# A Newton iteration with its cube formed from the other stationary operand, and without its symmetric step

## What is computed

```python
def iterative_inv(mat, n_iter=6):
    I = jnp.eye(m)
    K = mat
    denom = jnp.max(jnp.sum(K, axis=-2), axis=-1)[:, :, None, None]
    V = jnp.swapaxes(K, -1, -2) / denom
    for _ in range(n_iter):
        KV = jnp.matmul(K, V)
        V = jnp.matmul(0.25 * V, 13 * I - jnp.matmul(KV, 15 * I - jnp.matmul(KV, 7 * I - KV)))
    return V
SV = jnp.matmul(jnp.matmul(kernel1, iterative_inv(kernel2)), jnp.matmul(kernel3, V))
```

## Time and profile before

| what | value |
|---|---|
| median of three executions | 2761.87 us (2761.23 to 2764.32) |
| the profiled execution, its own time | 2772.52 us |
| its span, first to last instruction | 2770.8 us |
| TensorE matmul busy | 2229.7 us, 80% of the span |
| VectorE busy | 1893.1 us, 68% |
| ScalarE busy | 914.3 us, 33% |
| GpSimd busy | 797.3 us, 29% |
| mean granted TensorE clock | 0.937 of full speed |

### The profile page before, as it was taken

The page is one execution under the profiler, slowest core; times in us unless marked ns, Lnnn a source line. Parts: engine busy times, 40 slices in busy tenths (PEclk is TensorE's granted clock), DMA queues, the critical chain, the costliest instruction groups (busy, mean ns, idle before and its releaser), DMA issues.

```text
span 2770.8 us, 68027 instructions
## 1 busy us (share of the span) xinstructions
PE 2229.7 (80%) x28681; PEld 1674.0 (60%) x28681; DVE 1893.1 (68%) x4262; ACT 914.3 (33%) x2460; POOL 797.3 (29%) x831
## 2 busy tenths in 40 slices
PE   2998889889898777688888888888888888886775
PEld 2885555555687455466666666666666666664553
DVE  4666887887666899655666565665565665658996
ACT  1441000000244545333333333343343333334543
POOL 1004666766100222122222232222232222221221
PEclk9999999999999899789999999998999999987998
DMA  3000000000000000000000000000000000000002
GB/s 87 1 1 1 1 1 1 1 1 1 1 1 1 1 1 1 1 2 2 2 2 2 2 3 2 2 2 2 2 2 2 2 2 2 2 2 1 1 1 61
DMA packets 14559, 14.55 MB, mean 5 GB/s; under 512 B 1392, under 2 KB 12080, under 8 KB 14256
## 3 DMA queue, kind: packets, MB, share of 16 engines
q1 hardware_dynamic: 14256, 10.20, 1.3%
HBM read 6.01 MB, written 4.19 MB: 4 GB/s over the span
## 4 chain that ended last, share of the span: by engine, by line
PE 48%; DVE 29%; ACT 8%; issue 7%; POOL 6%; SPq 0%; DVEq 0%; POOLq 0%; DMA 0%
PE acc L683 6%; PE acc L466 5%; PE acc L1560 5%; PE acc L443 4%; PE acc L1549 4%; POOL arena L871 4%; DVE arena L835 3%; DVE arena L828 3%; ACT arena L1308 2%; PE acc L699 2%; DVE arena L838 2%; PE acc L1523 2%; ACT arena L884 2%; ACT arena L1327 2%; DVE arena L1159 2%
## 5 line engine op out<-in xcount | busy, mean ns | idle before, releaser
L1409 POOL TENSOR_TENSOR arena<-arena 128x288 f32<-128x288 f32 (+1 forms) x384 | 264.2, 705 | 878.0 <-ACT arena L1327 876.5
L630 POOL TENSOR_TENSOR arena<-arena,headcol 128x1024 f32<-128x1024 f32 x128 | 238.3, 1892 | 374.9 <-DVE arena L535 374.9
L683 PE MATMUL acc<-arena 128*128 128x512 f32 x512 | 269.4, 610 | 46.6 <-DVE arena L560 45.5
L1149 DVE SCALAR_TENSOR_TENSOR arena<-arena,acc 128x288 f32<-128x288 f32 (+1 forms) x384 | 154.4, 409 | 205.4 <-ACT arena L1327 196.2
L871 POOL TENSOR_TENSOR arena<-arena 128x960 f32<-128x960 f32 (+2 forms) x70 | 118.0, 1685 | 591.1 <-DVE arena L838 585.5
L1560 PE MATMUL acc<-arena 64*64 64x72 f32 x6144 | 244.4, 227 | 53.1 <-DVE arena L1149 51.9
L1560 PEld LDWEIGHTS acc<-arena 64*64 64x64 f32 x6144 | 218.5, 141 | 91.3 <-ACT arena L1327 71.3
L1549 PE MATMUL acc<-arena 64*64 64x72 f32 x6144 | 236.8, 228 | 9.5 <-DVE arena L1159 8.6
L1549 PEld LDWEIGHTS acc<-arena 64*64 64x64 f32 x6144 | 208.8, 135 | 48.3 <-issue 15.5
L1327 ACT ACTIVATE arena<-acc 128x288 f32<-128x288 f32 x384 | 150.4, 411 | 209.1 <-PE acc L1549 197.4
L1159 DVE SCALAR_TENSOR_TENSOR arena<-acc,arena 128x288 f32<-128x288 f32 (+1 forms) x384 | 151.5, 408 | 74.2 <-PE acc L1560 62.6
(11 more groups left out here) (230 smaller groups left out, 4495.3 us busy)
## 6 DMA issues: line engine op xcount, KB each, us to landing
out_dram<-X SPq DMA_DIRECT2D x4, 1024.0 KB, 9.3
wi<-in_wiT_dram SPq DMA_DIRECT2D x1, 256.0 KB, 2.7
wout<-in_woT_dram SPq DMA_DIRECT2D x1, 256.0 KB, 3.3
wqkv<-in_w_qkv_dram SPq DMA_DIRECT2D x1, 192.0 KB, 2.7
arena<-in_w_down_dram SPq DMA_DIRECT2D x1, 176.0 KB, 2.4
arena<-in_w_gate_dram SPq DMA_DIRECT2D x1, 128.0 KB, 2.2
arena<-in_w_up_dram SPq DMA_DIRECT2D x1, 128.0 KB, 2.7
wq<-in_WqT_dram SPq DMA_DIRECT2D x1, 64.0 KB, 2.2
```

The costliest lines, as they stand in the source:

```text
L630: pool.tensor_tensor(qx[s][:, q * NQ:(q + 1) * NQ, :], qkT[s][:, 0, :].unsqueeze(1).broadcast_to([P, NQ, SEQ]), headcol[:, q * NQ:(q + 1) ...
L683: pe.matmul(bank[s][1 + u % 2], qkT[s][:, 1, j * P:(j + 1) * P], qx[s][:, q * NQ:(q + 1) * NQ, j * P:(j + 1) * P], start=True, stop=True)\
L1409: pool.tensor_tensor(tm[s][:, group[g], cols], pm[s][:, group[g], cols], sq[s][:, group[g], cols], ALU.subtract).then_inc(tm_ready, 1)
```

## The change

The cube takes the remainder as stationary operand and streams the square past it. The step that makes P symmetric is left out on both engines, with its semaphore. The remainder no longer needs the eight columns W, so it is 64 columns wide in each of the six iterations, the last one too, where it was 72 in five and 8 in the last. GpSimd's `remainder` and VectorE's `newton` stay as they are. The constant `halfeye` is still made.

```diff
-            rm = [cut(NP, MW) for _ in R]
+            rm = [cut(NP, LM) for _ in R]
...
-            pstep = lambda n, it, g: (n * (NITER + 2) + it + (it >= EVEN)) * GR + g + 1
+            pstep = lambda n, it, g: (n * (NITER + 1) + it) * GR + g + 1
...
-                def even(n, s):
-                    for g in G:
-                        dve.wait_ge(p_ready, pstep(n, EVEN, g) - GR)
-                        dve.wait_ge(turn_done, n * GR + g + 1)
-                        dve.scalar_tensor_tensor(pm[s][:, group[g], 0:LM], pm[s][:, group[g], 0:LM], 0.5,
-                                                 pn[s][:, group[g], 0:LM], ALU.mult, ALU.add).then_inc(p_ready, 1)
-
                 def remainder(n, s, it):
 
-                    cols = slice(LM if it == NITER - 1 else 0, LM + HD)
                     for g in G:
 
                         dve.wait_ge(sq_ready, step(n, it, g))
                         dve.wait_ge(p_ready, pstep(n, it, g))
-                        dve.scalar_tensor_tensor(rm[s][:, group[g], cols], pm[s][:, group[g], cols], 7.0 * size[it],
-                                                 pn[s][:, group[g], cols], ALU.mult, ALU.subtract)\
+                        dve.scalar_tensor_tensor(rm[s][:, group[g], :], pm[s][:, group[g], 0:LM], 7.0 * size[it],
+                                                 pn[s][:, group[g], 0:LM], ALU.mult, ALU.subtract)\
                            .then_inc(rm_ready, 1)
...
                         newton(n, s, 2)
-                        even(n, s)
                         remainder(n, s, 3)
...
-                def symmetric(n, s):
-                    for g in G:
-                        pe.wait_ge(p_ready, pstep(n, EVEN, g) - GR)
-                        for p in range(g * PG, (g + 1) * PG):
-                            for rows, _ in halves:
-                                mm = pe.matmul(pn[s][rows, p, 0:LM], pm[s][rows, p, 0:LM], halfeye[rows, :],
-                                               start=True, stop=True, skip_group_check=True)
-                        mm.then_inc(turn_done, 1)
...
-                                mm = pe.matmul(pn[s][rows, p, cols], sq[s][rows, p, 0:LM], rm[s][rows, p, cols],
+                                mm = pe.matmul(pn[s][rows, p, cols], rm[s][rows, p, :], sq[s][rows, p, cols],
                                                start=True, stop=True, skip_group_check=True)
...
-                    if run:
-                        symmetric(n, s)
```

More of the change, by code:

```diff
@@ L1019, in nystrom @@
                      "rdc_ready", "p0_done", "p_ready", "sq_done", "sq_ready", "rm_ready", "tm_ready", "cube_done",
-                     "turn_done", "w_done", "wx_ready", "s1_done", "mx_ready", "mxT_done", "mxT_ready", "s1T_done",
+                     "w_done", "wx_ready", "s1_done", "mx_ready", "mxT_done", "mxT_ready", "s1T_done",
                      "e1_ready", "den_done", "num_done", "sv_ready", "y_done", "added")
@@ L1026, in nystrom @@
              rdc_ready, p0_done, p_ready, sq_done, sq_ready, rm_ready, tm_ready, cube_done,
-             turn_done, w_done, wx_ready, s1_done, mx_ready, mxT_done, mxT_ready, s1T_done,
+             w_done, wx_ready, s1_done, mx_ready, mxT_done, mxT_ready, s1T_done,
              e1_ready, den_done, num_done, sv_ready, y_done, added) = (sem(f"{ph}_{n}") for n in names)
```

## The result

The changed kernel takes 2834.4 us (median of four, 2818.25 to 2839.63; one further execution took 2793.16), beside 2761.55 us of the kernel before (four runs, 2760.11 to 2764.32). The changed kernel is slower, by something between 1.2 and 3.0%. Its times go with its mean granted clock: 2793.16 us at 0.911, 2818.25 at 0.901, 2834.89 at 0.893, 2839.63 at 0.890. The profiled execution took 2818.25 us. The forecast was 2730.8 us, range 2716 to 2776.

The account below looks back on a forecast made before the run. TensorE's in-order list was taken as the bound at the removed step. Gains of 33.6 and 5.3 us less 7.8 lost made 31.1 us, so 2761.87 us would become 2730.8, range 2716 to 2776.

Parts of the forecast that it names:

- TensorE's own list is the bound at the removed step; 1.07 us a turn.: Nyström phase, symmetric step: TensorE runs there without a pause, so dropping its 32 matmuls gains 33.6 us in all.
- The vector pass costs nothing.: VectorE's `even` in the symmetric step: 26.9 us busy, but it ran beside `totals`, so removing it was costed at nothing.
- The remainder, 5.3 us gained and 7.8 lost.: VectorE's remainder: narrower in iterations one to five gains 5.3 us; wider in the last, 0.25 later a turn, loses 7.8.
- The swap of operands costs nothing.: Cube: the stationary load already came after the wait for the remainder, so nothing; by the skill's rule 3 us worse.
- the sum: Gain over the Nyström turns: 33.6 + 5.3 - 7.8 = 31.1 us, taking the clock much like before.
- A clock much like before: Likeliest case: the summed gain with granted clock in the Nyström turns hardly changed, 2722 to 2742 us, chance 0.46.
- this sign: Prediction is wrong if the Nyström phase's mean granted clock, 0.93, falls clearly; then slow stretches exceed 6.8 us in many turns.
- the slow clock costs more than before: Rival: longer half-clock stretches behind TensorE's idle time; 11 turns with the long stretch, about 2772 us, chance 0.21.
- the alternation: Nyström turns before: short and middle slow stretches alternated nearly throughout; turns 1.0 us shorter would not fall into the same pattern.

Follow-up runs that it names:

- matmuls put back: Changed kernel with 32 matmuls that nothing reads at the symmetric step's place, without its vector pass: streaming 64 columns 2761.2 us, streaming 8 columns 2765.6 us.
- the kernel before with the fill: Kernel before with six matmuls of constants that nothing reads added ahead of `factors`: 2761.4 us, ratio 0.9988.

## Why the prediction was wrong

- *TensorE's own list is the bound at the removed step; 1.07 us a turn.* Right. The step left out alone has turns of 39.17 to 39.44 us at a clock of 0.96 beside 40.49, so 1.05 us and more.
- *The vector pass costs nothing.* Right: at a clock of 0.96 a turn takes 40.64 us with the matmuls back and without it, and 40.64 us with the operands swapped alone, which has it.
- *The remainder, 5.3 us gained and 7.8 lost.* Right within what can be told. Its 384 instructions of 256 elements take 420 ns, TensorE's idle time before `factors` grew from 66.5 us in 31 times (one of them in the earlier trace rows) to 74.8, 0.27 us each against 0.25 predicted, and the whole swap costs 0.13 us a turn against 0.08.
- *The swap of operands costs nothing.* Right within 0.05 us a turn: the run with it has turns of one clock 0.13 us longer, of which the sum put 0.08 down to the remainder's widths, and its fifth cube loads and streams as before. Its equal time, a ratio of 0.9996, says less, since the mix of its turns changed. The prediction set against this a rule of the Trainium skill ("TensorE: Matmul & The Clock Gate", "Step-by-step: what each phase is for"), that loads are pulled ahead of matmuls in flight. In neither order does the timeline show a load pulled across the wait at the fifth cube: it starts 0.03 us ahead of the stream in both. The loss priced there was 0.1 us a turn, 3 us in all; the turns leave room for half of that.
- *"A clock much like before", chance 0.46.* This is the step that failed: the sum took the same gain from each turn and put the change of the slow stretches at nothing. The equal clock sum of about 1 us a turn is confirmed by three pairs of kernels (39.55 and 40.49, and with the next clock 40.55 and 41.51; 36.77 and 37.73; 36.78 and 37.72), but the clock did not stay equal. In the profiled execution 18 turns cost 4.8 us and two 3.5 us over the short kind, and six 1.0: 99.4 us. Before, 14 turns at 1.0 and one at 3.7 made 17.7 us. The difference, 81.7 us, less 29 x 0.95 = 27.6 us, is 54 us, and the 29 turns together did become 1246.12 - 1192.1 = 54 us longer. The two profiled executions differ by less, 45.7 us, because that of the kernel before reached its first full turn 9 us later (1231.98 and 1223.02). The medians differ by more, 72.9 us; the other executions near 2834 us had a still lower clock (0.893), and there is no trace of them. The prediction had named this sign, that the granted clock of the phase falls clearly from 0.93: it fell to 0.85.
- *The rival "the slow clock costs more than before", chance 0.21.* This is what happened. Of its three reasons, that shorter turns leave the alternation is borne out by the step left out alone and by the matmuls put back; that TensorE has fewer matmuls is excluded only as to their streaming; the longer idle time is not the reason, since the kernel with the operands swapped has it and no long stretch, and the one with the step left out has long stretches without it. The argument against it, that nothing in the low stretch or just ahead of it loses matmuls, did not hold: time or matmuls put back 18 us ahead of the fall ended the long stretches. Nor does the clock always fall behind the idle time and the light matmuls: in the middle turn of the kernel before it fell at 1829.30, 0.45 us ahead of `factors`. Its size was wrong too. I let 11 turns take the long stretch of 13.7 us at 3.7; 18 took one of 17.1 us at 4.8 and two the one of 13.7. My range ended at 2776. That the alternation before was a favourable one, and that one length of turn could repeat for eleven turns with the worst stretch in each, stood in no row that I weighed.

What stays open is what exactly decides how long the clock stays at half. The runs show that both the time at which the weak stretch comes and the work in it matter, and that turns tend to settle at one length or a short cycle of lengths (40.5 and 41.5; 40.96; 44.35; 39.17, 43.16, 44.2 and 44.1). The operands swapped alone, the two kernels with matmuls put back and the kernel before with the fill average 40.93, 40.97, 40.99 and 40.96 us over 29 turns, and all four take 2761 to 2766 us, although their turns differ: there the mix of turns hides what an edit costs. The runs do not give a rule from which 2834 could have been worked out.

## What to carry to other kernels

Where every turn of a loop has a weak stretch of TensorE and the granted clock falls in it, compare turns of equal clock to see what an edit does, and treat the time of the whole as a second question: a microsecond less a turn cost 1 to 3% here, and gained 21 us once the weak stretch was filled. Fill the weak stretch first, by moving work that is ready into the wait, or by streaming more in instructions that are there anyway; then judge the edit. Matmuls of constants are less sure: they gained 124 us in one kernel and nothing in the other. A wait at the head of an in-order list is worth looking behind: `cube(5)` had its inputs for two microseconds while it stood behind `factors`.

## What the runs showed of the hardware

- Added work made a kernel faster by 73 us (matmuls that nothing reads), 100 us (unused columns) and 124 us (matmuls of constants). The granted clock over its 29 full turns rose from 0.85 to 0.94, 0.93 and 0.99.
- 32 matmul records of 64 by 64 that stream 72 columns take 1.22 us and those that stream 8 take 1.10, so between these widths the streamed columns are nearly free at full clock.
- Each matmul of the program shows as two records of the streaming and two of the load: the six fill matmuls are 12 records (x12). What the text ahead calls 32 matmuls, in the symmetric step as in `multiply` and `cube`, are 32 records and 16 matmuls of the program in each turn.
- A kernel's scatter can tell of the clock: the kernel before scatters by 0.2 to 0.4% in the three sets of 7 to 19 executions taken beside the experiments, with granted clocks of 0.938 to 0.944, and the changed kernel by 1.7%, with 0.890 to 0.911.
